# Second FFN pieces with ScalarE's copy and GpSimd's product, value products in pairs, the first norm four beats ahead

## The reference

```python
def norm(x, t, gw, gb, bw, bb):
    g = (t @ gw.T + gb)[:, None, :]
    b = (t @ bw.T + bb)[:, None, :]
    return g * x * lax.rsqrt(mean(x * x, axis=-1, keepdims=True) + 1e-6) + b
def block(x, t, ...):
    x = x + attention(norm(x, t, g1w, g1b, b1w, b1b), Wq, Wk, Wv, Wo)
    n = norm(x, t, g2w, g2b, b2w, b2b)
    return x + (silu(n @ gate_w.T) * (n @ hid_w.T)) @ out_w.T      # hidden width 512
out = x + block(x, cond_256, ...)
```

## Time and profile before

| | |
|---|---|
| median of three runs | 274.45 us (273.54 to 274.57) |
| the profiled execution | 273.25 us |
| its span | 271.2 us |
| TensorE, VectorE, ScalarE, GpSimd busy | 228.1, 204.4, 164.2, 111.9 us |
| mean granted TensorE clock | 0.956 |

### The profile page before, as it was taken

The page is one execution under the profiler, slowest core; times in us unless marked ns, Lnnn a source line. Parts: engine busy times, 40 slices in busy tenths (PEclk is TensorE's granted clock), DMA queues, the critical chain, the costliest instruction groups (busy, mean ns, idle before and its releaser), DMA issues.

```text
span 271.2 us, 8235 instructions
## 1 busy us (share of the span) xinstructions
PE 228.1 (84%) x3048; PEld 179.9 (66%) x3048; DVE 204.4 (75%) x489; ACT 164.2 (61%) x353; POOL 111.9 (41%) x183
## 2 busy tenths in 40 slices
PE   2436558977898999999999999999999899899895
PEld 2314236644666877787788778876887678677794
DVE  4655663497789798879887988888887888445573
ACT  5436373677586767775777677567656565565330
POOL 8244732173826272627262736252623232323320
PEclk9999755599999999999999999999999999999999
...
DMA packets 18818, 18.77 MB, mean 69 GB/s; under 512 B 3644, under 2 KB 17980, under 8 KB 18652
## 3 DMA queue, kind: packets, MB, share of 16 engines
...
...
## 4 chain that ended last, share of the span: by engine, by line
PE 40%; issue 29%; POOL 14%; DVE 11%; ACT 5%; POOLq 0%; ACTq 0%
PE pv L423 5%; PE proj L483 5%; PE ffn L317 4%; PE score L406 3%; DVE nmax L748 3%; PE ffn L319 3%; PE ffn L318 3%; PE tok L442 2%; POOL inv L910 2%; POOL xn_lo L923 2%; PE raw L379 2%; PE proj L345 2%; POOL inv L881 2%; PE tok L438 2%; POOL xs L916 2%
## 5 line engine op out<-in xcount | busy, mean ns | idle before, releaser
L748 DVE TENSOR_REDUCE nmax<-raw 128x8 f32<-128x1024 f32 x61 | 74.2, 1217 | 6.7 <-PE raw L379 6.6
L591 ACT ACTIVATE p_s<-score 128x1024 f32<-128x1024 f32 x64 | 65.5, 1023 | 15.7 <-PE score L406 14.5
L423 PE MATMUL pv<-p_s,va 128*32 128x128 f32 x1024 | 42.8, 287 | 0.9 <-ACT xn L609 0.4
L620 ACT ACTIVATE th<-ffn 128x256 f32<-128x256 f32 x53 | 20.3, 384 | 27.7 <-PE ffn L319 27.4
L317 PE MATMUL ffn<-xn_hi,ffn_hi 128*128 128x256 f32 x106 | 34.7, 327 | 0.0
L483 PE MATMUL proj<-ffn_out_s,hT 128*128 128x128 f32 x256 | 33.8, 275 | 0.3 <-DVE x_s L816 0.3
L805 DVE SCALAR_TENSOR_TENSOR gated<-th,ffn 128x256 f32<-128x256 f32 x53 | 22.0, 415 | 15.8 <-ACT th L620 15.5
L483 PEld LDWEIGHTS proj<-ffn_out_s,hT 128*128 128x128 f32 x256 | 31.2, 191 | 0.6 <-issue 0.5
L423 PEld LDWEIGHTS pv<-p_s,va 128*32 128x32 f32 x1024 | 25.2, 112 | 8.5 <-issue 3.2
L319 PE MATMUL ffn<-xn_hi,ffn_lo 128*128 128x256 f32 x106 | 29.7, 280 | 0.0
L318 PE MATMUL ffn<-xn_lo,ffn_hi 128*128 128x256 f32 x106 | 29.6, 279 | 0.0
...
## 6 DMA issues: line engine op xcount, KB each, us to landing
...
qs<-shift SPq DMA_DIRECT2D x64, 4.0 KB
...
```

The costliest lines, as they stand in the source:

```text
L423: mm = pe.matmul(pv[VW * j:VW * j + VW, (t % 2) * L:(t % 2 + 1) * L], va[vbuf(g)][:, t // 2, at:at + VW], p_s[:, (BEATS * g + t) % PBUF, p ...
L591: act.activation(p_s[:, n % PBUF, :], score[:], ACT.Exp, scale=SCALE).then_inc(s_exp, 1)
L748: dve.tensor_reduce(heads[:, :, t % 2, :], raw_dst(g, t)[:].rearrange("l (e j m) -> l e j m", e=HALVES, j=HQ), AX.X, ALU.max, negate=True) ...
```

## The change

Line numbers of the kernel after are some 10 to 45 higher (L341 for L330, L390 for L379, L419 for L406, L436 for L423, L451 for L438, L455 for L442).

- Odd pieces of groups 0 to 6 (28 of 64) are "pooled": ScalarE copies up, times 0.5, out of PSUM into `up` before it makes the tanh; VectorE makes `gated` alone; GpSimd makes `hT` = gated up (`d_hidden` on GpSimd, between the scaling and `d_resid` and `d_lo`). TensorE may overwrite the bank when `gated` is done. `gated` has a second buffer.
- Both value products of a batch stand in the even beat (`OT` = 2, where the second one stood already).
- `c_oT` stands before the tanh on ScalarE, and `a_mean` behind it.
- The first norm's squares and scaling of later groups stand four beats earlier (`MEAN` = -28), and those of group 3 in the prologue.
- In the prologue VectorE makes the zero fills of `va`; raw tiles 3 and 4 of group 0 and the transpose of the maxima stand before the transposes of group 2, which use two banks; `a_hi` and `lo_first` of group 0 and `a_hi` of group 1 stand earlier on VectorE, and `surround_values(0)` on GpSimd.

```diff
-    MEAN, XT1, HI1 = -24, -23, -15
+    MEAN, XT1, HI1 = -28, -23, -15
-    PV = 1
...
+        def pooled(n):
+            return n % 2 == 1 and n < PIECES * (G - 1)
...
@@ tensor: b_maxT, c_pv, d_gate_up, d_out
+                for f, i in due(T - 1, XT2, NB, 2):
+                    pe.wait_ge(s_xn2, NB * f + i + 1)
...
-                for f, i in due(T - 1, XT2, NB, 2):
+                for f, i in due(T - 2, XT2, NB, 2):
...
-                if 0 < n < SPREAD:
-                    pe.wait_ge(s_h, n)
-                elif SPREAD <= n < SPREAD + 2:
+                if SPREAD <= n < SPREAD + 2:
                     pe.wait_ge(s_max, BEATS * G)
-                elif n >= SPREAD + 2:
-                    pe.wait_ge(s_h, n - 2)
+                elif n > 0:
+                    last = n - 1 if n < SPREAD else n - 3
+                    if pooled(last):
+                        pe.wait_ge(s_gated, last + 1)
+                    else:
+                        pe.wait_ge(s_h, hidden_by_dve(last))
...
-                pe.wait_ge(s_h, PIECES * g + HC * w + 2 * half + 2)
+                n = PIECES * g + HC * w + 2 * half + 1
+                pe.wait_ge(s_h, hidden_by_dve(n))
+                pe.wait_ge(s_hp, hidden_by_pool(n))
@@ scalar: d_tanh
+                if pooled(n):
+                    if n > 1:
+                        act.wait_ge(s_hp, hidden_by_pool(n - 1))
+                    act.activation(up[:], ffn_dst(n)[:, PW:2 * PW], ACT.Copy, scale=0.5)
@@ scalar: prologue and beat
             a_mean(2)
-            zero_fill(va[0][:].rearrange("l b v -> l (b v)"), s_va0[0])
-            a_norm(2, 0)
-            a_norm(2, 1)
             a_values(0)
-            a_norm(2, 2)
-            a_norm(2, 3)
-            zero_fill(va[1][:].rearrange("l b v -> l (b v)"), s_va0[1])
+            a_mean(3)
+            for b in range(NB):
+                a_norm(2, b)
...
@@ gpsimd: d_hidden
+                pool.wait_ge(s_gated, n + 1)
+                if g > 0:
+                    pool.wait_ge(s_y, 2 * WIN * (g - 1) + 2 * w + ch // 2 + 1)
+                pool.tensor_tensor(hT[:, p, :], gated[:, 1, :], up[:], ALU.mult).then_inc(s_hp, 1)
```

84 lines of the change are left out of this document (55 added, 29 removed).

## The result

The kernel after takes 277.43 us (median of 4 runs, 277.4 to 278.32), the kernel before 274.0 in the same sitting (273.07 to 274.57): the ratio is 1.0136, interval 1.0098 to 1.0175. It is slower by 3.4 us where I forecast 5.6 faster, and the time lies outside my range. The profiled execution took 278.32 us with a span of 276.5, against 271.2 before.

A forecast was written before the change was run, and what follows sets the result against it. TensorE was taken as the bound, with about 2 us a group of waits on ScalarE and VectorE. Prologue -4.4 and six groups -1.2 gave -5.6, so 268.8 us from 274.45; range 262.0 to 273.5.

The forecast's parts named there:

- the terms -1.6, -1.4 and -1.26: Prologue: no gap in the first maxima -1.6, zero fills off ScalarE -1.4, group 3 scaled in the prologue -1.26 us.
- the pair's 1.0: Prologue at half clock: the second value product, now in beat 4, holds TensorE some 1.0 us longer.
- (b): Rival: half clock doesn't fall or rises some beats earlier, saving about 4 us, 264.8; chance 0.12.
- The earlier `oT_s`: Steady groups: making `oT_s` before the tanh gains 0.7 of the 1.2 us that the output projection waits.
- Saving by fewer changes of shape: Steady groups: pairing value products saves 0 to 0.15 us a pair, taken as 0.08, 0.3 a group.
- The stall at `c_tro`: Steady groups: TensorE reaches `c_tro` earlier and waits for `o_s`, 1.4 us instead of 0.55 a group: +0.85.
- The sum of these for a group without a first norm: Steady group: -0.7 - 0.3 + 0.85 + 0.3 = +0.15 us, with -0.2 taken.
- It is in the steady sum: First norm of later groups: square sum moved from beats 0 to behind the tanh in beats 4, given no separate term.
- The low parts behind the pooled product: GpSimd, odd pieces: TensorE waits 0.1 us at one window and 0.2 at the key, +0.3 a group.
- rival (c): GpSimd becomes the late engine: `d_lo` behind `d_hidden` delays each of 14 windows by a further 0.5, +7, 277.0; chance 0.09.
- nothing else changes: 0: Tail: odd beats lose about 0.6 us of `oT_s` wait, even beats gain 0.5, net 0.
- The port: Shared GpSimd/VectorE port: the sum of squares ends 0.42 us later beside the pooled product, 0.6 to 0.7 us in even beats.

The follow-up runs named there:

- prologue_only: Kernel before with only the change's prologue: no pooled pieces, single value products, first norm in beats 0, `oT_s` copy behind the tanh; 268.0 us, ratio 0.984.
- no_pool_unpaired: Kernel after with no piece pooled on GpSimd and each value product in the beat after its own score again; 260.9 us, ratio 0.958 to before.
- no_pool: Kernel after with no piece pooled on GpSimd, VectorE making both products of each piece again; 269.1 us, ratio 0.984 to before.
- inverse_late: Kernel after with low parts before the pooled product, single value products, and GpSimd's first-norm inverse and scaling at the end of beat 6; 258.9 us, ratio 0.950.
- spread_squares: Kernel after with low parts before the pooled product, single value products, and the first norm's four squares one each in beats 1 to 4; 257.8 us, ratio 0.945.
- norm_beat0: Kernel after with the later groups' first norm back in beat 0, its squares behind the tanh; 276.5 us, ratio 1.011 to before.
- lo_first_unpaired: Kernel after with the second norm's low parts before the pooled product on GpSimd and single value products again; 260.6 us, ratio 0.956 to before.
- lo_first: Kernel after with one step moved on GpSimd: the second norm's low part (`d_lo`) before the pooled product (`d_hidden`); 270.2 us, ratio 0.991 to before.
- spread_and_late: Kernel after with low parts before the pooled product, single value products, squares one each in beats 4 to 7, scaling at the end of beat 7; 260.6 us, ratio 0.955.
- unpaired: Kernel after with each value product in the beat after its own score again; 269.4 us, ratio 0.988 to before.
- lo_unp_beat6: Kernel after with low parts before the pooled product, single value products, and the first norm's squares and scaling in beats 6; 261.6 us, ratio 0.958.
- spread_inverse_late: Kernel after with low parts before the pooled product, single value products, squares one each in beats 1 to 4, scaling at the end of beat 6; 259.4 us, ratio 0.950.

## Why the prediction was wrong

**The prologue: right.** Up to score 3 the terms -1.6, -1.4 and -1.26 say -4.3, and -4.4 is measured: score 0 came 1.4 earlier, score 1 a further 1.4, and scores 2 and 3 together a further 1.6. At score 10, without the pair of value products, the sum said -5.4, and prologue_only has -5.7. What I had not thought of is that the half clock may come more than once. In the kernel after there were two more falls before score 10, and score 10 stands 2.2 us later than in prologue_only (66.99 against 64.84); some of that is the pair's 1.0, which I had. The two are not separated. That a denser prologue could be followed by more falls was in no rival; (b) knew only a gain. Its price, 4 us for the stage of 23.9, was too high: three executions of the kernel before whose mean granted clock was 1.0 took 271.1, 271.1 and 271.9, 1.6 to 2.5 under the median of their sitting, and no_pool_unpaired took 260.8 at 0.954 and 261.0 at 0.998.

**The earlier `oT_s`: right in kind, too small.** I took 0.7 of 1.2 us; prologue_only against no_pool_unpaired shows 1.2 in a group without a first norm. Beat 1 gave 0.80 (I had 0.6) and beat 3 gave 0.46, which is the 0.4 that I read off ScalarE's rows; I had taken 0.3 of it back for TensorE coming there earlier, which it does only in pairs (with them, in no_pool, it waits 0.41 in beat 3 for `oT_s`).

**The pairing: the step that failed in every group.** Saving by fewer changes of shape: two single products hold TensorE for 2 x 0.58 us, a pair for 134.19 - 133.18 = 1.01, so 0.15 a pair, the upper end of my 0 to 0.15. The stall at `c_tro` I put at +0.85 a group. It was forecast rightly where I saw it, 1.05 in beats 6 to 7, measured 0.99 at 145.46. But that the odd beats get back what the even ones give was an error. From no_pool_unpaired to no_pool, in the group without a first norm, the gate product of every even beat starts 1.56 us after its score instead of 1.13: four times 0.43 added. `c_tro` starts 0.75 after the score instead of 1.13 in beats 1 and 5, 0.92 instead of 1.13 in beat 3, and at 1.6 in both in beat 7: about 1.0 taken back. In beats 1, 5 and 7 the end of `o_s` keeps its distance to the score (0.7, 0.7 and 1.5), so `c_tro` can't come earlier than that, whatever stands in front of it; and beat 3 has the 0.41 of waiting for `oT_s` again. The net cost is 1.2 us in a group without a first norm (26.2 to 27.4), where I had -0.3 + 0.85 = +0.55.

**The sum of these for a group without a first norm was right by luck.** It was +0.15, of which I made -0.2; before has 27.37 and 27.15, after 27.63 and 27.20. The early copy gave 0.5 more and the pairing took 0.65 more.

**The first norm: the step that was missing.** "It is in the steady sum" was the whole of my working on it, and there was no term for it. 1.2 us of ScalarE and 2.1 of GpSimd were moved into beat 4, and cost 1.1 (beats 5 and 6 of no_pool_unpaired, 3.81 and 3.09 against 3.44 and 2.35) to 1.3 in each of three groups. `p_s`, `xn` and the query's low part follow directly there. Nor had I noticed that `a_transpose` waits for the exponential that frees `score`, which is how the delay reaches TensorE. inverse_late and spread_squares show both halves: GpSimd's queue makes beat 6 longer and ScalarE's beat 5. In its old place, beat 0 ahead of the tanh, the first norm cost 0.2; norm_beat0 put it in beat 0 behind the tanh and paid 1.4, so it doesn't tell what the old place would cost now.

**The low parts behind the pooled product: right in mechanism, wrong in size.** I had +0.3 a group and, as rival (c), a further 0.5 for each window, at 0.09. My sign for it stood in the prediction: groups over 28.2, then look at what `d_lo` waits for. A group without a first norm lost 0.2, as by my sum; with one 0.7 to 0.9, mostly in beat 6, because GpSimd came to the product late, not because `gated` was late; and the tail 3.2, where I had "nothing else changes: 0". In the tail beats are paced by the chain through tanh and `gated`, so a queue behind `gated` costs the whole wait, 2.25 here, and the clock at half speed came on top of it.

**The port: right in kind, too large in size.** The sum of squares, 0.29 before, now takes 0.516 in the median, where I had 0.6 to 0.7, and up to 0.728 beside the pooled product (by line: min/median/max ns; kernel after, first as grouped, then one with the product beside it):

```profile
L807 DVE CUSTOM_DVE_ANT_0 sqx<-x x32: 292/516/728, 46.6 to 258.9; 128x128 f32<-128x128 f32 x32
```

```profile
132.53 0.73 POOL L964 TENSOR_TENSOR hT<-gated,up 128x256 f32<-128x256 f32 x1
...
132.69 0.72 DVE L807 CUSTOM_DVE_ANT_0 sqx<-x 128x128 f32<-128x128 f32 x1
```

What pooling takes from VectorE is 28 products of 0.42, 11.8 us. In the kernel after the sum of squares took back 5.6 of it (by line, 17.7 against 12.1 us for 32), half of what I had. Between no_pool_unpaired and lo_first_unpaired VectorE's busy time differs by 3.5 only (204.2 and 200.7): there most was taken back, 4.9 us by the sum of squares (15.6 against 10.7) and 2.2 by the casts to `xn_hi` of the first norm (6.2 against 4.0). That the rest is worth nothing is what their equal times show.

In the sum, against the terms as they were forecast: three groups with a first norm 5.7 more (+5.1 for -0.6), the two without 0.7, beats 50 to 62 0.4, the tail 3.2, score 10 0.9. That is 10.9, and -5.6 + 10.9 = 5.3 is the difference of the two spans, 276.5 and 271.2; the medians differ by 3.4, since the profiled execution of after was 0.9 over its median and that of before 0.75 under the median of its sitting. Rival (c), at 277.0, named nearly the right time and one of the right places, in part by luck: it spread 7 us evenly over 14 windows, and 3.2 of what came stood in a single one, in the tail; the cost of the first norm, which stood in no case, made up for what the other windows lacked.

## What to carry to other kernels

Moving a step to another beat, or to another side of a wait in the same beat, needs a term of its own in the sum, even where its work stays the same: list for each engine what stands right behind the new place and when its result is due. Here four squares cost 0.2 us a group ahead of the tanh of beat 0, 1.4 behind it, and 1.1 in beat 4. On an engine that works strictly in order, put a step that waits for a long chain behind the short steps that others wait for; and price such a queue where the pace is set by the chain (in the tail above all), not only where the bound engine hides it. Putting two products side by side saved 0.15 us of TensorE a pair and still cost 0.3, since it put 0.43 in front of a chain that paced the beat after. And a kernel that is changed in five places at once should be taken apart: the prologue alone gave 5.3 us here, and the whole lost 3.4.

## What the runs showed of the chip

The half clock is less fixed than I took it to be, and it isn't a property of the kernel: executions of one kernel differ in it. In the first sitting the kernel before had mean granted clocks from 0.925 to 1.0, and no_pool_unpaired from 0.954 to 0.998. So what follows is told of one profiled execution of each kernel, and no edit is shown to set it. The first stage at half clock lasted 23.9 us in before and after and in five others (lo_first, lo_first_unpaired, no_pool_unpaired, prologue_only, spread_and_late), but 10.2 us in unpaired, norm_beat0, inverse_late, lo_unp_beat6, spread_inverse_late and spread_squares, which had a second one of 10.2; no_pool had a single stage, of 3.4. Later stages lasted 3.4 or 6.8 otherwise. Before a fall TensorE had been busy for 1.15, 1.97 and 2.11 of 3.40 us in the kernel after.

The tail is the clearest case. After, norm_beat0 and unpaired are the three kernels in which TensorE waits 2.2 us for the low part there, and in all three the clock fell 0.5 to 1.2 us after that wait ended, for 3.4 us in which TensorE was busy throughout. In none of the others did it fall between score 63 and the end of TensorE's work. From score 63 to the end these three took 27.1 to 27.6 us, the others 23.6 to 24.6. So a stall can cost more than its own length: with the low parts first the tail was 3.3 us shorter than in after and 3.5 shorter than in unpaired, for a wait of 2.2.
